# A two-block audio tower on one core: row maxima subtracted in four wide products, and the padded copies of x in another place of ScalarE's queue

## What is computed

```python
h = tok(x)                                    # (32, 64, 256): silu(x W_h + b_h) W_o + x W_r ...
# attention on xn = layernorm(h)
xh = xn.reshape(b, s, 16, 16)
q, k, v = xh Wq', xh Wk', xh Wv'
energy = einsum('bqhd,bkhd->bhqk', q, k) / sqrt(256)
attn = softmax(energy)                        # the row maximum is subtracted before exp
h = h + (attn v) @ W_out.T + b_out
# feed-forward: a product with a fixed spectrum
h = h + real(ifft(fft(layernorm(h)) @ w)) + bias
```

## Time and profile before

| | us |
|---|---|
| median of 3 runs (140.0 to 140.31) | 140.23 |
| the profiled execution's own time | 140.08 |
| its span in the trace | 138.2 |
| PE busy | 132.4 (96%) |
| DVE / POOL / ACT busy | 111.3 / 95.0 / 85.6 |
| share of PE in the chain that ended last | 87% |

### The profile page before, as it was taken

How to read it: one execution, slowest core, us unless ns; L and a number is a source line. 1 busy time by engine, 2 the same in 40 slices (tenths; PEclk the granted TensorE clock), 3 DMA queues, 4 the chain that set the end, 5 groups by cost and what they waited for, 6 DMA issues and landing times.

```text
span 138.2 us, 6119 instructions
## 1 busy us (share of the span) xinstructions
PE 132.4 (96%) x2443; PEld 111.5 (81%) x2443; DVE 111.3 (81%) x337; ACT 85.6 (62%) x245; POOL 95.0 (69%) x186
## 2 busy tenths in 40 slices
PE   6799999999999999999999999999999999999991
PEld 2489999999988787978878889888788897887650
DVE  5695497679978579898898898988989989879671
ACT  5467475478868585864947748659476485662410
POOL 3384699998547274678687696886876968674750
PEclk9999999999999999999999999999999999999998
DMA  4577100120000020120312303213123031121012
GB/s 68 157 176 230 55 0 0 14 33 2 0 0 5 0 24 5 19 52 14 64 38 24 62 0 62 48 16 66 39 24 60 2 62 46 15 57 47 5 38 76
DMA packets 24508, 5.89 MB, mean 43 GB/s; under 512 B 20384, under 2 KB 24224, under 8 KB 24480
## 3 DMA queue, kind: packets, MB, share of 16 engines
q1 hardware_dynamic: 24192, 5.37, 18.5%
q10 hardware_dynamic: 288, 0.13, 0.4%
HBM read 2.35 MB, written 2.10 MB: 32 GB/s over the span
## 4 chain that ended last, share of the span: by engine, by line
PE 87%; DVE 4%; ACT 4%; issue 1%; ACTq 1%; POOL 0%; DVEq 0%; POOLq 0%
PE bank L1067 11%; PE bank L973 10%; PE bank L1053 7%; PE bank L1109 6%; PE bank L1129 6%; PE bank L978 5%; PE bank L1162 5%; PE bank L1116 5%; PE bank L1097 4%; PE bank L967 3%; PE bank L1175 3%; PE bank L1080 2%; PE bank L1166 2%; PE bank L1133 2%; PE bank L1184 2%; PE bank L1154 2%
## 5 line engine op out<-in xcount | busy, mean ns | idle before, releaser
L830 DVE TENSOR_REDUCE bank<-bank 128x4 f32<-128x256 f32 x64 | 22.8, 425 | 6.8 <-ACT pT L377 6.3
L377 ACT ACTIVATE pT<-bank 128x256 f32<-128x256 f32 x64 | 19.4, 393 | 2.6 <-PE bank L1080 2.5
L1067 PEld LDWEIGHTS bank<-qT,xzT 32*128 32x128 f32 x512 | 15.7, 186 | 2.7 <-issue 2.7
L1067 PE MATMUL bank<-qT,xzT 32*128 32x64 f32 x512 | 17.9, 276 | 0.0
L702 DVE TENSOR_TENSOR hid_lo<-bank,hid_hi 128x512 fp32r<-128x512 f32 x16 | 11.0, 686 | 7.3 <-ACT bank L342 7.1
L588 POOL TENSOR_TENSOR side_lo<-sideT,side_hi 128x256 fp32r<-128x256 f32 x14 | 10.2, 729 | 7.9 <-ACT sideT L388 7.9
L549 POOL TENSOR_SCALAR xblk<-xh,parity_sb 128x128 f32<-128x128 f32 x32 | 11.6, 375 | 5.8 <-PE bank L1116 4.6
L372 ACT ACTIVATE maxT<-bank 128x128 fp32r<-128x128 f32 x16 | 4.4, 278 | 17.7 <-PE bank L1089 17.7
L599 POOL TENSOR_TENSOR on_lo<-onT,on_hi 128x256 fp32r<-128x256 f32 x14 | 10.3, 738 | 7.1 <-ACT on_hi L392 6.9
L557 POOL TENSOR_TENSOR hb_all<-h_all,bout_bc 128x256 f32<-128x256 f32 x16 | 11.6, 734 | 3.9 <-ACT h_all L346 3.9
L341 ACT ACTIVATE hid_hi<-bank 128x512 fp32r<-128x512 f32 x16 | 9.6, 599 | 5.0 <-PE bank L967 5.0
(11 more groups left out here) (170 smaller groups left out, 380.8 us busy)
## 6 DMA issues: line engine op xcount, KB each, us to landing
out<-y SPq DMA_DIRECT2D x16, 128.0 KB, 1.7
xblk<-xh SPq DMA_DIRECT2D x32, 32.0 KB, 2.3
wo_raw<-in_W_o SPq DMA_DIRECT2D x1, 512.0 KB, 3.9
wout_raw<-in_W_out SPq DMA_DIRECT2D x1, 256.0 KB, 3.0
fr<-in_wr SPq DMA_DIRECT2D x1, 256.0 KB, 4.6
fi<-in_wi SPq DMA_DIRECT2D x1, 256.0 KB, 4.7
minus_raw<-in_minus_rows SPq DMA_DIRECT2D x1, 128.0 KB, 2.1
bout_bc<-in_b_out SPq DMA_DIRECT2D x1, 128.0 KB, 4.1
```

Of the source, the lines that this page charges most:

```text
L377: nc.scalar.activation(pT[:, j, :], bank[j][:, D:2 * D], ACT.Exp).then_inc(exp_done, 1)
L830: nc.vector.tensor_reduce(rowmax[:, j, :], bank[j][:, 0:D].rearrange("p (h k) -> p h k", k=TOK), AX_X, ALU.max).then_inc(max_done, 1)
L1067: pe.matmul(bank[j][:, at0:at0 + TOK], xzT[t % 3][rows32, 2 * half + b, :, :].rearrange("p e k -> p (e k)"), qT[t % 3][rows32, half, TOK * ...
```

## The change

Three edits. **take_max** becomes four products of 256 columns, one for each row group. For that `maxT` is 128 x 2 x 128: two copies of the transposed maxima, each scaled by a per-partition 0 or 1 (two new columns of `parity`), so that each half of the heads finds only its own rows; ScalarE makes two copies instead of one. `minus_rows` becomes one 128 x 128 matrix instead of two; its load and its conversion on GpSimd are half as large.

**copy_xzT** moves on ScalarE from behind `copy_xT` to behind `copy_q`, the last thing of a step, and now waits for `x_lo_set`. VectorE's `split_x` waits for x_hi (`xT_copied`), and for xzT only in its first two tiles; `split_x(2)` moves ahead of the maxima of tile 0. Since xzT now reads X_BANK last, `turn_x(t)` on TensorE waits for `xzT_copied` as well.

**scores_inputs** moves on TensorE from the head of the step to just before `scores`.

```diff
@@ -42,9 +42,9 @@
     sine[0] = np.cos(np.pi * n[0])
     r = np.arange(P)
     head_blocks = (r[:, None] // HD == r[None, :] // HD).astype(np.float32)
-    parity = (np.stack([r // HD % 2, r // HD % 2, r // TOK, r // TOK], 1) == [0, 1, 0, 1]).astype(np.float32)
-    head_of = 2 * np.arange(HALF)[:, None] + np.arange(P)[None, :] // TOK
-    minus_rows = np.where((r[:, None, None] % 32 < 8) & (r[:, None, None] % 4 == head_of[None]), -1.0, 0.0).astype(np.float32)
+    parity = (np.stack([r // HD % 2, r // HD % 2, r // TOK, r // TOK, r % 4 // 2, r % 4 // 2], 1)
+              == [0, 1, 0, 1, 0, 1]).astype(np.float32)
+    minus_rows = np.where((r[:, None] % 32 < 8) & (r[:, None] % 2 == r[None, :] // TOK), -1.0, 0.0).astype(np.float32)
     pair_ones = (r[:, None] // TOK == np.arange(32)[None, :] // HD).astype(np.float32)
     return {
         "identity": np.eye(P, dtype=np.float32),
@@ -73,7 +73,7 @@
         ident = sb("ident", [P, P])
         ident16 = sb("ident16", [P, P], BF16)
         blocks = sb("blocks", [P, P])
-        parity = sb("parity_sb", [P, 4])
+        parity = sb("parity_sb", [P, 6])
         cosine = sb("cosine_sb", [P, D])
         sine = sb("sine_sb", [P, D])
         bh = sb("bh", [P, NC])
@@ -136,11 +136,11 @@
         x_lo = sb("x_lo", [P, D], F32R)
         xzT = [sb(f"xzT{i}", [P, 2 * HALF, 2, TOK]) for i in range(3)]
         qT = [sb(f"qT{i}", [P, HALF, P]) for i in range(3)]
-        minus_raw = sb("minus_raw", [P, HALF, P])
-        minus_rows = sb("minus_rows_sb", [P, HALF, P], F32R)
+        minus_raw = sb("minus_raw", [P, P])
+        minus_rows = sb("minus_rows_sb", [P, P], F32R)
         pair_ones = sb("pair_ones_sb", [P, 32])
         max_terms = sb("max_terms", [P, QUADS, 32], F32R)
-        maxT = sb("maxT", [P, P], F32R)
+        maxT = sb("maxT", [P, HALF, P], F32R)
         pT = sb("pT", [P, QUADS, D])
         sumsT = sb("sumsT", [P, D])
         inv_sum = sb("inv_sum", [P, D // 32, 2])
@@ -358,6 +358,7 @@
                 nc.scalar.activation(x_hi[:], bank[X_BANK][:, 0:D], ACT.Copy).then_inc(xT_copied, 1)
 
             def copy_xzT(t):
+                act.wait_ge(x_lo_set, t + 1)
                 for e in range(2):
                     nc.scalar.activation(xzT[t % 3][:, :, e, :], bank[X_BANK][:, 0:D].rearrange("p (g k) -> p g k", k=TOK),
                                          ACT.Copy, scale=parity[:, e:e + 1]).then_inc(xzT_copied, 1)
@@ -369,7 +370,9 @@
 
             def copy_max(t):
                 act.wait_ge(max_turned, t + 1)
-                nc.scalar.activation(maxT[:], bank[MAX_BANK][:, 0:P], ACT.Copy).then_inc(max_copied, 1)
+                for half in range(HALF):
+                    nc.scalar.activation(maxT[:, half, :], bank[MAX_BANK][:, 0:P], ACT.Copy,
+                                         scale=parity[:, 4 + half:5 + half]).then_inc(max_copied, 1)
 
             def exponent(t):
                 for j in range(QUADS):
@@ -405,13 +408,13 @@
                     copy_side(i - 1)
                 if i + 3 < T:
                     copy_xT(i + 3)
-                    copy_xzT(i + 3)
                 if i < WHOLE_ON:
                     lead_on(i)
                 if i + 1 < T:
                     exponent(i + 1)
                 if i + 3 < T:
                     copy_q(i + 3)
+                    copy_xzT(i + 3)
 
             def keep_value_weights():
                 act.wait_ge(value_copied, 1)
@@ -780,7 +783,9 @@
                                             parity[:, e:e + 1], None, ALU.mult).then_inc(xzT_copied, 1)
 
             def split_x(t):
-                dve.wait_ge(xzT_copied, 2 * (t + 1))
+                if t < 2:
+                    dve.wait_ge(xzT_copied, 2 * (t + 1))
+                dve.wait_ge(xT_copied, t + 1)
                 nc.vector.tensor_tensor(x_lo[:], bank[X_BANK][:, 0:D], x_hi[:].bitcast(F32),
                                         ALU.subtract).then_inc(x_lo_set, 1)
 
@@ -902,11 +907,11 @@
                 if 1 <= i < T - 2:
                     finish(i - 1)
 
+            split_x(2)
             dve.wait_ge(zeros_set, 3)
             for j in range(QUADS):
                 maximum(0, j)
             split_max(0)
-            split_x(2)
             h_stats(T - 2)
             h_stats(T - 1)
             variance1(3)
@@ -1071,16 +1076,14 @@
 
             def take_max(t):
 
-                pe.wait_ge(max_copied, t + 1)
+                pe.wait_ge(max_copied, HALF * (t + 1))
                 if t == 0:
                     pe.wait_ge(minus_set, 1)
-                for half in range(HALF):
-                    for j in range(QUADS):
-                        rows32 = slice(32 * j, 32 * j + 32)
-                        last = pe.matmul(bank[j][:, D + half * P:D + (half + 1) * P], minus_rows[rows32, half, :],
-                                         maxT[rows32, :], start=False, stop=(half == HALF - 1), skip_group_check=True)
-                        if half == HALF - 1:
-                            last.then_inc(keyed_done, 1)
+                for j in range(QUADS):
+                    rows32 = slice(32 * j, 32 * j + 32)
+                    pe.matmul(bank[j][:, D:2 * D], minus_rows[rows32, :],
+                              maxT[rows32, :, :].rearrange("p h q -> p (h q)"),
+                              start=False, stop=True, skip_group_check=True).then_inc(keyed_done, 1)
 
             def turn_max(t):
                 pe.wait_ge(max_lo_set, t + 1)
@@ -1171,6 +1174,7 @@
                 pe.wait_ge(xh_set, t + 1)
                 if t >= 1:
                     pe.wait_ge(q_copied, t)
+                    pe.wait_ge(xzT_copied, 2 * t)
                 for half in range(HALF):
                     last = pe.transpose(bank[X_BANK][:, half * P:(half + 1) * P], xh[t % 2][:, half * P:(half + 1) * P],
                                         ident[:])
@@ -1206,8 +1210,6 @@
                 pe.matmul(half, halfway[:, 1, c * P:(c + 1) * P], sine[:], start=False, stop=True).then_inc(mixw_done, 1)
 
             def step(i):
-                if 0 <= i + 2 < T:
-                    scores_inputs(i + 2)
                 if i == 1:
                     turn_x(4)
                 if i >= 1:
@@ -1217,6 +1219,7 @@
                 if 0 <= i < T - 3 and i != 1:
                     turn_x(i + 3)
                 if 0 <= i + 2 < T:
+                    scores_inputs(i + 2)
                     scores(i + 2)
                 if 0 <= i + 1 < T:
                     keyed_scores(i + 1)
```

## The result

Median of 22 runs: 140.56 us (139.94 to 142.7), against 140.37 (139.95 to 140.6) for 22 runs of the kernel before beside them. The forecast was 138.8, with a range of 138.2 to 139.9. The profiled execution took 140.13, span 138.3; before it was 140.08 and 138.2.

A forecast was written before the change was run, and what follows sets the result against it. TensorE's queue was taken to bound each 5.56 us step. Early steps +0.05 and -0.15, 13 tiles at -0.10 and -0.07 at the end gave -1.47 from 140.23: 138.8 us, range 138.2 to 139.9.

The forecast's parts named there:

- s: TensorE time saved per tile in take_max by one pack of wide products instead of two: 0.10 us, ends 0 and 0.13.
- rival 1: In take_max, columns cost what they count: s only 0.05 to 0.06, so 139.3 us; chance 0.14.
- The padded copies: ScalarE's xzT copies, awaited by turn_x, were forecast just in time for its weight load, margin 0.06 us.
- d: Lateness per step of the xzT copies at turn_x's load: taken as 0, with 0.05 as the range's end.
- Rival 2: xzT copies late by 0.03 to 0.10 us at turn_x's load in steps 2 to 12: 139.1 to 139.9; chance 0.13.
- rival 4: ScalarE's three copies behind the query don't overlap, turn_x's load 0.20 late eleven times: 141.2 us; chance 0.06.
- maxT's second copy: Extra ScalarE copy of the maxima: 0.25 us a step, upper end 0.36, covered by idle time and later slack.
- The early steps: First steps: s of tiles 0 and 1 lost plus 0.05, then 0.15 gained; together -0.10 beside tile 2's s.
- 3 to 4: From tile 3's scores load to tile 4's: 0.15 us gained because xh is no longer late, beside s.
- 2 to 3: From tile 2's scores load to tile 3's: turn_x(4) waits for padded copies, costing 0.05 us and losing early s.
- The rule for the load: In step 1, turn_x(4)'s load comes 1.49 us behind the query's start, at 54.09 less the s of tile 0.
- The last step: Kernel end: s of tiles 13 and 14 stays on the path, 0.07 us of tile 15's counts.

The follow-up runs named there:

- e2: Changed kernel with only the wide take_max products and two maxT copies, copy_xzT and waits as in the kernel before: 144.13 us, ratio 1.0276.
- e3: Changed kernel with only the moves (copy_xzT, scores_inputs, split_x(2)); maxima in eight products and one maxT copy as before: 140.66 us, ratio 1.0025.
- e11: Changed kernel with maxima subtracted from only 128 of 256 columns, so its output differs: one run, 139.72 us.
- e4: Changed kernel with ScalarE's copies side_hi and sideT put ahead of the two copies of the maxima: 140.85 us, ratio 1.0042.
- e5: Changed kernel with the two waits of VectorE's first two split_x joined to one each: one run, 139.27 us.
- e1: The changed kernel measured again without any edit: 140.3 us (139.54 to 142.35), ratio 0.9999 to the kernel before.
- e8: Changed kernel with the transposes of x of tile 4 behind those of h and the maxima in step 1: one run, 140.45 us.
- e6: Changed kernel with TensorE's nine idle products at the start cut into four each, 54 more recorded instructions: 139.83 us, ratio 0.996.
- e7: Changed kernel with four buffers for y instead of two: 139.64 us, ratio 0.9958.

## Why the prediction was wrong

**Bounds and mechanism: right.** TensorE's queue sets the step, the step is uniform from tile 5 on, and the wide products shorten it only with the move (`e2`, `e3`).

**The size of s: wrong, half.** The term is "s = 0.10"; it measured 0.05 to 0.06 (0.30 instead of 0.36; 5.51 instead of 5.56), which is rival 1, given 0.14. The step that failed: "the wider one is not longer, so the fp32r product of 128 columns keeps the array about as long as one of 256". The recorded length of a product, 0.27 to 0.28 for both widths, is not how long it holds the array. Starts are: the query's three products of 256 columns, each recorded as 0.27 to 0.28, start 0.11 to 0.12 apart. `e11` shows the price directly. The Trainium skill, page "Perfetto Trace Analysis", section "Summary: the profiler window per engine type", says that TensorE's recorded end is estimated. The Trainium skill, page "TensorE: Matmul & The Clock Gate", section "Back-to-back issue gap", gives N/2.4 + 2.5 ns for a single isolated product, so 53 ns for 128 more columns (an estimate from that formula); the 0.05 to 0.07 here agree, for four row groups at once. For a sustained stream of weight loads and products the same section gives 81 ns at 128 columns and 131 at 512, some 17 ns for 128 more (an estimate from these two), and `e11` speaks against that. I had weighed the first rule and went by the recorded lengths. The miss is worth 13 times 0.05, so 0.6 us.

**The padded copies: right.** d = 0; they end 0.11 ahead of the load, the forecast's 0.05 of hand-over and 0.06 of margin. Rival 2 and rival 4, ScalarE's copies one after another, are out: two xzT take 0.83.

**maxT's second copy: right that it is covered**, a little dearer: side_hi starts 0.52 behind maxT instead of 0.17, 0.35 instead of 0.25. `e4` shows that this costs the step nothing.

**The early steps: half right.** "3 to 4" did lose its 0.15, beside s. "2 to 3" was forecast at some +0.05 and became +0.24. The rule for the load (1.49 behind the query's start) holds to 0.06: 52.84 + 1.49 = 54.33, measured 54.39. What failed is "less the s of tile 0": the gain of take_max is used up before the query, since TensorE waits there for on_lo:

```profile
52.27 0.30 PEld L1169 LDWEIGHTS bank<-value_hi,on_lo 128*128 128x128 f32 x2 [0.22 <-POOL on_lo L602]
...
54.39 0.20 PEld L1179 LDWEIGHTS bank<-ident,xh 128*128 128x128 f32 x2 [0.41 <-issue]
```

GpSimd has mix_lo ahead of on_lo there, 1.27 us that only this step has. It was so before the change, a wait that the prediction doesn't have: on_lo was done at 51.24 + 0.73 = 51.97, and the load that takes it started at 52.02.

```profile
51.24 0.73 POOL L599 TENSOR_TENSOR on_lo<-onT,on_hi 128x256 fp32r<-128x256 f32 x1
...
52.02 0.30 PEld L1166 LDWEIGHTS bank<-value_hi,on_lo 128*128 128x128 f32 x2
```

**Not foreseen: 0.2 at "4 to 5".** No step of the prediction looked at where instructions lie in an engine's stream. `e5` shows it.

**Not foreseen, and the largest: the end.** "The last step" counts only take_max and takes the stores as they were, at nothing and without a reason. A kernel with 64 products fewer has its code loaded at other moments, and the last load fell on the one store that a y waits for. In five of the seven traces with 64 products fewer and no edit of the end (after, `e1`, `e2`, `e4`, `e8`; not `e5`, `e11`) one of the last stores landed after 3.0 to 3.8 us: tile 13's in after, `e1`, `e2` and `e8`, the last one in `e4`. What it cost can be read in the column "end": 17.1 to 17.9 where tile 13's was held, against 16.8, so 0.3 to 1.1; 18.4 in `e4`, most of it the last store. In the medians it is 140.56 or 140.3 against 139.6 to 139.8 in `e6` and `e7`: 0.5 to 0.9.

The account, from 140.37: the steps give -0.46 (the forecast had some -1.4; of the difference 0.6 is s, 0.19 is "2 to 3" and 0.22 "4 to 5", less 0.1 for "1 to 2", which gained unforeseen); the held store +0.5 to +0.9. That leaves 140.4 to 140.8; measured 140.56. Without the held store the steps alone would give 139.9; `e6` and `e7` ran at 139.83 and 139.64, and what the remaining 0.1 to 0.3 is, no run shows. Rival 1 had put the change at 139.3.

**Open.** Why instruction 191 of VectorE is late. Why "1 to 2" gained 0.13 (`e2` alone has 0.05 of it, `e3` 0.07). Why the place of tile 0's scores varies by 0.7 us from one execution to the next in either kernel: the runs of the kernel before lie mostly from 139.95 to 140.25 or from 140.4 to 140.6, which such a difference would explain, but no run was made on it. What sets the moment of the last load: in after, `e1`, `e2` and `e8` it came behind 2373 or 2374 of the 2379 products (133.05 to 136.44 us) and met tile 13's store, in `e4`, `e5` and `e11` behind the last one (137.18, 138.29 and 139.08), where it met the last store (`e4`) or none, though TensorE has as many products in all seven. That decides whether a run of the changed kernel is hit.

## What to carry to other kernels

Take what a product costs from how far apart the starts of its kind are, never from its recorded length. When a change removes or adds instructions, look at the instruction rows of the DMA queues: count to the place of the last code load and see what transfers will be under way there, above all where a buffer's reuse waits for a store. And when medians stand still while the lowest run falls and the highest rises, two effects are at work; look for the one that strikes only some runs.

## What the runs showed of the chip

- TensorE's code comes in packets of 16 KB, 19 in this kernel, one for about every 260 recorded instructions; each holds one DMA engine for 0.9 to 1.6 us. A store of 128 KB has eight packets on each engine and lands mostly in 1.7, at most in 2.4, but in 3.0 to 3.8 when such a load comes ahead of its packets on one engine (ten stores in seven of the 13 traces).
- A place in VectorE's stream, recorded instruction 191 counted from 0, starts late in all 13 traces (all but `e7`'s): 0.08 to 0.09 behind the end of the instruction ahead in the six where it is y, 0.29 to 0.30 in the seven where it is h. In the steady steps both start 0.05 to 0.08 before that end. Counted from the end of recorded instruction 190, a semaphore instruction in all 13, it is 0.40 to 0.42 for either.
- 128 more columns in four row groups at once cost 0.05 to 0.07 us; the recorded product grows too (359 ns in the mean instead of 285), but not in a way from which that could be read.
